# Where the token rows are scattered to the experts: from three stretches of each batch to two

## The reference

```python
xn = layernorm(x)                                   # (4, 2048, 256)
# branch s, per batch
Q, K, V = (layer_norm(xn @ W + b) for W in (Wq, Wk, Wv))
phiQ, phiK = tanh(Q @ Wphi_q + b) + 1, tanh(K @ Wphi_k + b) + 1
alpha = softmax(mean(Q) . K over the rows) * L      # needs all rows of the batch
KV, K_sum = sum of (phiK * alpha) x V, of phiK * alpha
attn = layer_norm(conv5(num / den) + ...)           # per row tile
s = attn + gelu(attn @ W1 + b1) @ W2 + b2 + xn
# branch g, mixture of experts
probs = softmax(ln2 @ router.T);  top_p, top_i = top_k(probs, 2)
buf[expert, pos] = ln2[token]                       # the scatter, capacity 1280
g = hidden + gate * (gelu(buf @ w1) @ w2)[expert, pos]
```

## Time and profile before

| | us |
|---|---|
| median of 3 runs | 2003.02 |
| lowest, highest | 2002.83, 2003.76 |
| the profiled execution | 2004.66 |
| its span, first to last instruction | 2002.9 |

### The profile page before, as it was taken

One profiled execution on the slowest core, in us unless ns is written; L12 is line 12 of the kernel. 1 busy time (PEld: TensorE's weight loads), 2 busy tenths in 40 slices (PEclk: granted clock), 3 DMA queues, 4 the chain that ended last, 5 costly groups with the idle time before them and its releaser, 6 DMA issues. The chain is left out here.

```text
span 2002.9 us, 37020 instructions
## 1 busy us (share of the span) xinstructions
PE 1805.4 (90%) x12775; PEld 1616.6 (81%) x12776; DVE 1370.3 (68%) x3444; ACT 814.7 (41%) x1946; POOL 1064.7 (53%) x1499
## 2 busy tenths in 40 slices
PE   3899996398998999997999999999969899999998
PEld 2676775285898867996999999999956799885998
DVE  3988884754555545555878888887746577684676
ACT  1566663273323553232333333333346234472332
POOL 3666552675555565553678787787643133340431
PEclk9999997598999998998999999999989999998999
DMA  7555522123222122122455555644334011240110
GB/s 207 158 179 178 169 93 81 48 74 122 73 71 82 63 93 79 62 67 88 105 102 120 106 133 102 125 103 80 54 92 127 22 39 43 80 135 24 33 48 30
DMA packets 175285, 184.74 MB, mean 92 GB/s; under 512 B 25107, under 2 KB 166719, under 8 KB 175118
## 3 DMA queue, kind: packets, MB, share of 16 engines
q1 hardware_dynamic: 136990, 133.05, 21.9%
q0 software_dynamic: 33824, 49.51, 11.4%
q10 hardware_dynamic: 4304, 0.02, 0.1%
HBM read 98.16 MB, written 90.44 MB: 94 GB/s over the span
## 5 line engine op out<-in xcount | busy, mean ns | idle before, releaser
L1863 POOL DMA_INDIRECT after_d<-h,home x160 | 259.3, 1621 | 107.4 <-DVE h L1914 62.7
L1783 ACT ACTIVATE hid<-bank 128x512 f32<-128x512 f32 x160 | 95.7, 598 | 335.8 <-PE bank L129 335.8
L127 PE MATMUL bank<-rows_hi,up_hi 128*128 128x256 f32 x640 | 188.8, 295 | 12.9 <-DVE rows_lo L1907 8.1
L129 PE MATMUL bank<-rows_hi,up_lo 128*128 128x256 f32 x640 | 181.8, 284 | 0.0
L128 PE MATMUL bank<-rows_lo,up_hi 128*128 128x256 f32 x640 | 181.8, 284 | 0.0
L127 PE MATMUL bank<-down_hi,hid_hi 128*128 128x256 f32 x640 | 181.1, 283 | 0.0
L128 PE MATMUL bank<-down_lo,hid_hi 128*128 128x256 f32 x640 | 181.1, 283 | 0.0
L129 PE MATMUL bank<-down_hi,hid_lo 128*128 128x256 f32 x640 | 181.0, 283 | 0.0
L1202 POOL DMA_INDIRECT buf_d<-rows_in,to_row x128 | 134.8, 1053 | 86.5 <-POOL rows_in L1198 42.4
L1184 POOL TENSOR_SCALAR cnorm<-cmv 128x1 f32<-128x1 f32 x64 | 15.3, 239 | 278.7 <-DVE cmv L1695 277.7
L1930 DVE TENSOR_TENSOR hid_lo<-hid,hid_hi 128x512 fp32r<-128x512 f32 x160 | 132.6, 843 | 39.8 <-ACT hid_hi L1783 37.2
(11 more groups left out here) (321 smaller groups left out, 5566.4 us busy)
## 6 DMA issues: line engine op xcount, KB each, us to landing
buf_d<-zeros SPq DMA_DIRECT2D x16, 1360.0 KB, 7.4
rows_in<-buf_d SPq DMA_DIRECT2D x80, 272.0 KB, 3.2
rows_in<-ln_d SPq DMA_DIRECT2D x128, 128.0 KB, 2.1
x<-in_x SPq DMA_DIRECT2D x16, 512.0 KB, 4.1
after_d<-after SPq DMA_DIRECT2D x16, 512.0 KB, 2.9
ln_d<-ln SPq DMA_DIRECT2D x16, 512.0 KB, 2.9
xa<-in_x SPq DMA_DIRECT2D x16, 512.0 KB, 4.3
up_w<-in_w_t POOLq DMA_DIRECT2D x16, 512.0 KB, 4.1
```

The costliest lines, as they stand in the source:

```text
L127: pe.matmul(dst, hi, mhi, start=start and i == 0, stop=False)
L129: mm = pe.matmul(dst, lo, mhi, start=False, stop=end)
L1783: act.activation(dst[:, 2 * half:2 * half + 2].rearrange("p f c -> p (f c)"), bank[half][:], ACT.Gelu_apprx_tanh).then_inc(e_hid, 1)
L1863: pool.indirect_dma_start(after_d, bass.IndirectOffsetOnAxis(home[i % TAG_RING][:, r:r + 1], axis=0), h2[p][:, r], None, bounds_check=T - ...
```

## The change

`amid` becomes tiles 0 to 15. The first loop issues no scatter, the middle sixteen, and the second loop the last sixteen: also with tiles 0 to 3 of the convolution. SP's loads follow the same order. `attend(2)` has no scatters and stays as it is.

```diff
@@ -1032,8 +1032,7 @@
-                soon = range(BT // 2) if scatters else range(BT)
-                amid = range(BT // 2, EACH - BT + 4) if scatters else ()
+                amid = range(EACH - BT) if scatters else ()
@@ -1128,13 +1127,13 @@
                                 load_x(b, 3)
-                                for j in (*range(2, BT // 2), *amid):
+                                for j in amid[2:]:
                                     load_tile(job_of(b, j))
                                 if b == first:
                                     load_x(b + 1, 0)
                                     load_x(b + 1, 1)
                                 for i in range(SECOND_STEPS):
-                                    if 4 <= i < BT:
+                                    if i < BT:
                                         load_tile(job_of(b, EACH - BT + i))
@@ -1215,8 +1214,6 @@
                             if i % GROUP == 0 and i // GROUP + 1 < GROUPS:
                                 norm_x(b, i // GROUP + 1)
-                            if scatters and i % 2 and i < BT:
-                                scatter(job_of(b, i // 2))
 
                         def middle(b):
                             for j in amid:
@@ -1228,7 +1225,7 @@
-                            if scatters and 4 <= k < BT:
+                            if scatters and 0 <= k < BT:
                                 scatter(job_of(b, EACH - BT + k))
```

## The result

The changed kernel takes 2029.34 us (median of 4 runs, 2025.91 to 2034.11), the kernel before 2002.92 (4 runs, 1996.36 to 2003.76): the ratio is 1.0148, 95% interval 1.0124 to 1.0172, slower by 1.5%. On the ratio that is 29.6 us, where 28.1 were forecast. The medians differ by 26.4 us, and the profiled executions by 27.9 us of span, 2030.8 against 2002.9.

What follows compares the result with a forecast made beforehand. PE, busy in 90% of the span, was the bound; POOL counts only where PE waits. -11.2 + (13.7 + 9.5) + (5.3 + 5.3 + 1.2) + 1.3 + 3.0 = +28.1 us gave 2031.1 us, range 2020 to 2043.

Steps and rivals of the forecast that it cites:

- First loops: First Q and K transposes to first phi-of-Q product, batches 0 and 1: without eight scatters each, -7.1 and -4.05, together -11.2 us.
- The middles: Sixteen scatters in place of twelve take 63.7 and 60.8 us; POOL reaches the second loop 13.7 and 9.5 us late.
- Start of the second loop: Four added scatters: first up product 15.95 us behind the first root, where today it is 10.7; +5.3 us in each batch.
- The loads of x: Batch 0, end of the middle: two 512 KB loads delay tile 16's load and scatter, +1.2 us, between 0 and 4.
- Tile 3's normalisation amid the gelus: Second loop: tile 3's root is ready 5.1 us behind the up product's begin, ACT wants it at 3.8; +1.3 us together.
- The clock: Beginning of the second loop's up products: PE at half speed costs 0 to 3 us a batch, 1.5 taken, +3.0 us.
- the half clock lasts through all the up products: Rival, first pair of tiles in the second loop: 5.7 us a batch lost in place of 1.5, 2039.5 us; chance 0.12.
- all else: Costed at nothing: SP's reordered loads, and the experts' begin, since the last scatter stays at tile 15 of batch 1.
- the low end of the range: All low ends together: 3.65 us a tile, POOL late by 8.4 and 7.0, no clock loss, -12; gives 2018 us.
- the pace is POOL's own: Rival, middles: loads keep ahead, 3.3 us a tile, sixteen take 53.4, POOL late by 3.4 and 2.0; 2013.3 us; chance 0.06.
- made up later: Rival, rest of the second loop: PE catches up on the lateness; half of it returned gives about 2014 us; chance 0.06.
- POOL's scatters do not hold the roots: Rival, start of the second loop: added scatters can be passed, only the first loops' gain is left, 1991.8 us; chance 0.03.

Runs made afterwards that it cites:

- the early scatters alone: Against the kernel before: four scatters in each first loop, twelve in each middle, sixteen in each second loop; ratio 1.0032 (1.0017 to 1.0047).

## Why the prediction was right, point by point

**First loops.** Forecast -11.2, measured -11.5, and the run that leaves those scatters out has the same 61.0 us loops. The batches without scatters were a true measure of PE's own pace.

**The middles.** Forecast 63.7 and 60.8 us for sixteen scatters and a first root 13.7 and 9.5 us late; measured 63.0 and 62.4 us, 13.2 and 11.1 late. Taking each batch's own mean was finer than the trace allows: over three profiles of the changed program's middles (63.0, 61.9, 61.9 in batch 0 and 62.4, 61.1, 63.6 in batch 1) the two don't differ. In the slack itself, 44.6 against 46.0 us, the batches differed in the clock: ahead of batch 1's first root it was 0.50 for 4 us, ahead of batch 0's it was 1.00. That the pace is the round trip of two buffers is shown by the third buffer. The estimate by the Trainium skill (DMA: Bandwidth & Descriptors, Anatomy of one DMA), 61.6 us, lies within a few per cent of all of these. The Trainium skill gives the fit there for DMAs that GpSimd issues, and the tile loads are SP's; in the middle of batch 0 the changed kernel's profile has a median of 2.2 us to landing for the loads and 2.7 for the scatters, near the 2.3 that the estimate took for both. The Trainium skill's advice to issue early and wait late (Rules for kernel authors) was borne out: with two buffers in the middle 15.5 us of POOL's time went into waiting for loads.

**Start of the second loop.** Forecast +5.3 a batch, measured +5.1 in batch 1 and +5.2 in both batches of the run with the early scatters alone.

**The loads of x.** Forecast 1.2 us in batch 0, measured 2.8: the term was mis-sized within its bounds (0 to 4). I had counted the next load's issue as late by what the earlier trace rows shows; in the changed kernel the scatter of tile 14, for which that load waits, landed only at about 519 us beside one megabyte of x, 2 us behind the middle's last scatter, and the wait for the load was 3.11 us.

**Tile 3's normalisation amid the gelus.** Forecast 1.3 us together, up to 1.3 a batch. In batch 0 of the changed kernel the first down product comes 10.58 us behind the first up product, where the kernel before has 8.89: 1.7 us. The clock is not the reason there, it was 1.00 in the six microseconds behind the up product. ACT waits for tile 3's root in the midst of the gelus, where the earlier trace rows has it at once, and takes the tile up 5.9 us behind the up product where I had 5.1; timeline of ACT in the changed kernel, batch 0:

```profile
541.44 0.56 ACT L1329 ACTIVATE tk<-bank,cnorm 128x256 f32<-128x256 f32 x1 [2.01 <-POOL cnorm L1186]
```

I had counted half of too small a bound, and had not seen that this term and the next overlap.

**The clock.** Forecast +3.0, 1.5 a batch, at the beginning of the up products. Ahead of them half speed cost nothing, as forecast, since PE waits for POOL's steps of 6.5 us (15.7 us in batch 1, where 15.95 were forecast at full clock). Behind the first up product it depends on the batch. In batch 0 the clock was full again and cost nothing. In batch 1 the granted clock was 0.72 in the first 6 us, and the first down product came 10.66 us behind the up product, as late as in batch 0 but for another reason: ACT waited 1.63 us for the up products and only 0.51 us for tile 3's root, and PE had no idle time ahead of the down product. Timeline of ACT in the changed kernel, batch 1:

```profile
825.44 0.84 ACT L1365 ACTIVATE tk<-bank,b1c 128x256 f32<-128x256 f32 x2 [1.63 <-PE bank L129]
826.78 0.56 ACT L1329 ACTIVATE tk<-bank,cnorm 128x256 f32<-128x256 f32 x1 [0.51 <-POOL cnorm L1186]
```

So either of the two takes 1.2 to 2.0 us from the first pair of tiles, and they do not add up: 3.5 us in both batches together, where the two terms of the forecast have 4.3. Over the five profiles with early scatters (the changed kernel twice, with three buffers, with the loads of x later, and the early scatters alone) five of ten batches had half clock behind the first up product. The rival that the half clock lasts through all the up products, 5.7 us a batch, was met in none: the clock was full again within some 5 us of the first up product.

Another 2.3 us came at the turn from batch 0 to 1, where one of PE's products behind a wait for gelus took 0.58 us, with a granted clock of 0.91 over the stretch, and none over 0.39 in the kernel before (line 1532, the bias of the down products). The changed kernel with three buffers has the same order there and 34.8 us for the stretch, as the kernel before, so the change does not force it; what decides it stays open.

**The sum.** The terms, forecast and measured in the profiled executions: first loops -11.2 and -11.5; lateness of the first root 23.2 and 24.3; early scatters 10.6 and 10.1; loads of x 1.2 and 2.8; tile 3 and the clock 4.3, and 3.0 for the whole rest of the second loops; all else 0 and -0.8. That is 28.1 and 27.9. The large terms were right by their mechanism. That the sum came out to 0.2 us is luck, since single terms are off by up to 1.6 us and the time of one execution varies by several. Nor was the low end of the range the one that the bounds give: it takes 3.65 us a tile, for which no row is named, where the bound of 3.3 us would give about 2008.

The rival "the pace is POOL's own" is what three buffers give, to 2 us; for two it was rightly priced as unlikely. The rival "made up later" has nothing for it, the rest of the second loops got longer. The rival "POOL's scatters do not hold the roots" has fallen with the roots 6.57 us apart and the 5.2 us a batch of the early scatters.

## What to carry to other kernels

Idle time of an in-order engine is worth something only where no one waits for what comes behind: a gap between two chains takes as many items as fit into it at their real pace, and each one more is paid in full. The pace in a gap isn't that in a loop, where other work hides the transfers' round trip; with two buffers a back-to-back stretch is paced by latency, and a third buffer changes nothing until that stretch is the one that ends last. When a program has a twin stage without the work in question, its trace is the best price list.

## What the runs showed of the hardware that I had not expected

Two 512 KB loads hold up a scatter in flight beside them: it took 6.3 us to land where the median is 2.7, the tile load that waited for it was issued 7.0 us behind them, and moving them took 2.5 us off. And half clock was free while the work was paced by another engine's 6.5 us steps, 15.7 us from the first root to the first up product with it (batch 1 of the changed kernel) and 15.9 at a granted clock of 1.00 (the early scatters alone). Where PE's own work was waited for, it cost 1.8 us at the start of the loop, and 1.2 us and more in the up products behind the early scatters, where tile 3's root would have cost as much.
